# A layer of Fourier attention and a quantized feed-forward: another order of the opening, and one constant made on the chip

## The reference

```python
x = x + attn(layernorm(x), W_q, W_kv, W_o)        # x: 4 x 512 rows of 512
x = x + ffn(layernorm(x), gate_w, up_w, down_w, gate_scale, up_scale, down_scale)

def attn(x, W_q, W_kv, W_o):                      # 16 heads of 32
    qf  = l2_normalize(fft((x @ W_q.T).reshape(B, S, 16, 32)))
    kvf = l2_normalize(fft((x @ W_kv.T).reshape(B, S, 16, 32)))
    kvf = cumsum(kvf, axis=1)                     # over the rows
    return ifft(qf * kvf).real.reshape(B, S, 512) @ W_o.T

def ffn(x, ...):                                  # 512 -> 1536 -> 512, weights cast to fp8
    fuse = silu(x @ q(gate_w) * gate_scale) * (x @ q(up_w) * up_scale)
    return fuse @ q(down_w) * down_scale
```

## Time and profile before

| | us |
|---|---|
| median of 3 runs | 419.12 |
| lowest and highest | 418.77, 419.37 |
| the profiled execution | 419.79 |
| its span in the trace | 418.0 |

### The profile page before, as it was taken

How to read it: one execution, slowest core, us unless ns; L and a number is a source line. 1 busy time by engine, 2 the same in 40 slices (tenths; PEclk the granted TensorE clock), 3 DMA queues, 4 the chain that set the end, 5 groups by cost and what they waited for, 6 DMA issues and landing times.

```text
span 418.0 us, 5504 instructions
## 1 busy us (share of the span) xinstructions
PE 408.8 (98%) x1897; PEld 202.8 (49%) x1897; DVE 297.4 (71%) x514; ACT 193.2 (46%) x323; POOL 108.2 (26%) x114
## 2 busy tenths in 40 slices
PE   7999999999999999999999999999999999999994
PEld 3744454445555554454555555454444444444442
DVE  4998998999999699997984972167865854422234
ACT  3687756587736245445242563255442441131220
POOL 0133551015154137043541012032461001300003
PEclk9999999999999999999999999999999999999998
DMA  8986546600181143232112014411112051200002
GB/s 249 264 267 239 163 117 162 149 17 2 38 256 36 26 77 71 57 127 74 28 26 50 2 29 101 72 50 53 26 26 52 0 77 25 100 2 0 2 0 101
DMA packets 57547, 33.55 MB, mean 80 GB/s; under 512 B 49456, under 2 KB 49840, under 8 KB 57392
## 3 DMA queue, kind: packets, MB, share of 16 engines
q1 hardware_dynamic: 57088, 32.93, 30.3%
q10 hardware_dynamic: 432, 0.28, 0.2%
HBM read 17.44 MB, written 4.19 MB: 52 GB/s over the span
## 4 chain that ended last, share of the span: by engine, by line
PE 89%; DMA 3%; DVE 3%; ACT 2%; POOL 1%; SPq 1%; issue 1%; POOLq 0%; DVEq 0%
PE bd L488 20%; PE bu L470 19%; PE bg L470 19%; PE ba L370 14%; PE ba L415 8%; PE bd L370 3%; DMA h<-x_dram 1%; PE ba L388 1%; PE bd L415 1%; DMA hT<-w_q_dram 1%; PE bd L388 1%; PE bd L356 1%; PE bu L415 1%; POOL xs L1603 1%; PE bg L447 0%
## 5 line engine op out<-in xcount | busy, mean ns | idle before, releaser
L470 PE MATMUL bu<-hT,gu 128*128 128x512 f16 x384 | 90.7, 379 | 0.0
L470 PE MATMUL bg<-hT,gu 128*128 128x512 f16 x376 | 89.0, 379 | 0.0
L1234 DVE SCALAR_TENSOR_TENSOR ff<-bu,us,sl 128x512 f32<-128x512 f32 x48 | 35.9, 748 | 56.0 <-PE bu L470 52.8
L741 ACT ACTIVATE sl<-bg,gs 128x512 f32<-128x512 f32 x48 | 32.9, 686 | 78.0 <-PE bg L470 77.0
L370 PE MATMUL ba<-wf,xT 128*128 128x512 f16 x288 | 63.2, 379 | 0.0
L470 PEld LDWEIGHTS bu<-hT,gu 128*128 128x128 f16 x384 | 37.5, 98 | 45.5 <-DVE ff L1234 0.6
L470 PEld LDWEIGHTS bg<-hT,gu 128*128 128x128 f16 x376 | 35.6, 98 | 44.9 <-issue 4.1
L488 PE MATMUL bd<-dw,fu 128*128 128x512 f32 x192 | 51.1, 411 | 0.0
L1634 POOL TENSOR_TENSOR h<-ff,h 128x512 f32<-128x512 f32 x14 | 17.5, 1272 | 122.2 <-DVE ff L1265 122.2
L370 PEld LDWEIGHTS ba<-wf,xT 128*128 128x128 f16 x288 | 27.9, 98 | 34.1 <-issue 1.1
L488 PE MATMUL bd<-own,half 128*128 128x512 f16 x184 | 43.0, 379 | 0.0
(11 more groups left out here) (201 smaller groups left out, 524.3 us busy)
## 6 DMA issues: line engine op xcount, KB each, us to landing
h<-x_dram SPq DMA_DIRECT2D x16, 256.0 KB, 4.2
out_dram<-h SPq DMA_DIRECT2D x15, 256.0 KB, 2.0
hT<-w_q_dram SPq DMA_DIRECT2D x4, 256.0 KB, 5.0
gu<-w_kv_dram SPq DMA_DIRECT2D x4, 256.0 KB, 4.4
hT<-gate_w_dram SPq DMA_DIRECT2D x2, 512.0 KB, 3.5
hT<-up_w_dram SPq DMA_DIRECT2D x2, 512.0 KB, 5.6
gu<-woT_dram SPq DMA_DIRECT2D x1, 1024.0 KB, 5.1
hT<-down_w_dram SPq DMA_DIRECT2D x2, 512.0 KB, 4.9
```

Of the source, the lines that this page charges most:

```text
L470: m = e.matmul(bk[:, :], gu[:, c, 4 * w + k, col:col + P], hT[:, b % 2, part, k, :], start=k == 0 and part == 0, stop=k == KT - 1 and part ...
L741: e.activation(sl[:, n % 2, :], bg[:, :], ACT.Silu, scale=gs[:, i:i + 1]).then_inc(a_silu, 1)
L1234: e.scalar_tensor_tensor(out=ff[:, n % 2, :], in0=bu[:, :], scalar=(us if b < HALF else us2)[:, i:i + 1], in1=sl[:, n % 2, :], op0=ALU.mul ...
```

## The change

- **TensorE** folds the second query block ahead of `heads(0, 1)`; the last two query blocks are folded together, bank by bank (`pe_fold_last`), so that banks become complete one after the other. Two key blocks are folded ahead of `heads(1, 1)`. The warm-ups become 14, 3, 3, 3 and 3 instead of 14, 3 and 4.
- **VectorE** takes the second pair's scaling ahead of tile 1's statistics, and the sums and scalings of the key weights, with the low parts of the query weights, ahead of `xn(0, 1)` and of tile 2's statistics. It writes the constant `heads` with five memsets (`dve_heads`); `fwd` alone is read from memory.
- **ScalarE** sums block 5 and copies the first folded bank ahead of tile 1's root; `act_xh(0, 1)` goes behind the sum of block 7. A wait is added for a buffer of `act_sum_w`.
- **SyncE** issues x's tile 2 behind all blocks of the key weights, whose last two change places; the constant's transfer is 64 KB instead of 128 KB.

```diff
-            return 7 * w + KT + k
+            return 10 + k if w else 3 + k

             if j == 0:
-                e.wait_ge(d_cst, 16)
+                e.wait_ge(v_heads, 5)

+        def pe_fold_last(e):
+            for f in (2, 3):
+                e.wait_ge(v_head, 3 + f)
+            for k in range(KT):
+                for f in (2, 3):
+                    m = e.matmul(ba[AT["fold", 0, k]][:, P * f:P * f + P], raw[0][:, f, P * k:P * k + P], fs[:, f, :],
+                                 start=True, stop=True)
+                m.then_inc(s_fold, 1)

@@ tensor_program
             pe_heads(e, 0, 0)
             pe_warm(e, 3)
             pe_fold(e, 0, 0)
+            pe_fold(e, 0, 1)
             pe_heads(e, 0, 1)
-            pe_warm(e, 4)
-            pe_fold(e, 0, 1)
-            pe_fold(e, 0, 2)
-            pe_fold(e, 0, 3)
+            pe_warm(e, 3)
+            pe_fold_last(e)
             pe_heads(e, 1, 0)
             pe_qk(e, 0, 0, 0)
-            pe_heads(e, 1, 1)
+            pe_warm(e, 3)
             pe_fold(e, 1, 0)
             pe_fold(e, 1, 1)
+            pe_heads(e, 1, 1)
+            pe_warm(e, 3)
             pe_fold(e, 1, 2)
             pe_fold(e, 1, 3)
             pe_qk(e, 0, 1, 0)

@@ act_sum_w
+            if j > KT:
+                e.wait_ge(*summed(j - KT))

@@ scalar_program
             act_sum_w(e, 3)
+            act_sum_w(e, 5)
+            act_wf(e, 0, 0)
             act_root0(e, 0, [1])
-            act_sum_w(e, 5)
-            act_xh(e, 0, 1)
-            act_wf(e, 0, 0)
             act_wf(e, 0, 1)
             act_wf(e, 0, 2)
             act_wf(e, 0, 3)
             act_sum_w(e, 7)
+            act_xh(e, 0, 1)
             act_root0(e, 0, [2])

@@ dve_head
+            if j == 0:
+                e.wait_ge(d_cst, 16)

+        def dve_heads(e):
+            e.memset(heads, 0.0).then_inc(v_heads, 1)
+            e.wait_ge(v_heads, 1)
+            for q in range(4):
+                r = slice(HD * q, HD * q + HD)
+                e.memset(cst[r, 128 + HD * q:128 + HD * q + HD], 1.0 / UNIT).then_inc(v_heads, 1)

@@ vector_program
             dve_zero(e)
+            dve_heads(e)
...
             dve_sum_w(e, 2)
+            dve_head(e, 0, 1)
             dve_stats1(e, 0, 1)
             dve_root0_head(e, 0, [1])
-            dve_head(e, 0, 1)
+            dve_wf(e, 0, 0)
+            dve_wf(e, 0, 1)
+            dve_sum_w(e, 4)
+            dve_wf(e, 0, 2)
+            dve_wf(e, 0, 3)
+            dve_head(e, 1, 0)
             dve_root0_tail(e, 0, [1])
             dve_xn(e, 0, 1)
+            dve_sum_w(e, 6)
+            dve_head(e, 1, 1)
             dve_stats1(e, 0, 2)
-            dve_sum_w(e, 4)
-            dve_wf(e, 0, 0)
-            dve_wf(e, 0, 1)
-            dve_wf(e, 0, 2)
-            dve_wf(e, 0, 3)
-            dve_sum_w(e, 6)
-            dve_head(e, 1, 0)
+            dve_root0_head(e, 0, [2])
             dve_stats1(e, 0, 3)
-            dve_root0_head(e, 0, [2])
-            dve_head(e, 1, 1)
             dve_root0_tail(e, 0, [2])

@@ sp_cst
-            e.dma_start(cst[:, 0:256], cst_d).then_inc(d_cst, 16)
+            e.dma_start(fwd, cst_d).then_inc(d_cst, 16)

@@ sync_program
             sp_raw(e, 1, 1)
-            sp_x(e, 0, 2)
             sp_raw(e, 1, 0)
             sp_xT(e, 0, 0)
+            sp_raw(e, 1, 3)
             sp_raw(e, 1, 2)
-            sp_raw(e, 1, 3)
+            sp_x(e, 0, 2)
             sp_ident(e)
```

More of the change, by code:

```diff
@@ L40, in constants @@
         inv[r, r] = np.concatenate([ire, iim], 1)
-    heads = np.kron(np.eye(4), np.ones((HD, HD))) / 2.0 ** 14
     ident = np.eye(P)
@@ L44, in constants @@
     ones = np.ones((P, P))
-    return (np.concatenate([fwd, heads, ident], 1).astype(np.float32),
+    return (np.concatenate([fwd, ident], 1).astype(np.float32),
             np.concatenate([inv, tri, ones], 1).astype(np.float32))
+UNIT = 2.0 ** 14
 NPR = 18
@@ L197, in build @@
         a_zh, v_zl = sem("act_zh"), sem("dve_zl")
+        v_heads = sem("dve_heads")
         v_most, s_bound, a_bound, v_unit2, v_gus, p_dw = (
@@ L1929 @@
         "ds": np.ascontiguousarray(L0_ffn_down_scale),
-        "cst": np.ascontiguousarray(cst[:, 0:2 * P]),
+        "cst": np.ascontiguousarray(cst[:, 0:P]),
         "cst2": cst2,
-        "ident": np.ascontiguousarray(cst[:, 2 * P:]),
+        "ident": np.ascontiguousarray(cst[:, P:]),
     }
```

## The result

| | before | after |
|---|---|---|
| median of 4 runs, us | 418.94 | 423.82 |
| lowest and highest | 418.40, 419.37 | 423.46, 424.41 |
| the profiled execution | 419.79 | 424.41 |
| its span | 418.0 | 422.6 |

The kernel is slower by a ratio of 1.0104 (95% interval 1.0083 to 1.0125), some 4.4 us; the forecast was 422.4 in a range of 420.3 to 424.6. The two medians in the table lie 4.9 us apart: the ratios given here with an interval are estimated from the single executions and are not quotients of two medians. A second set, six executions of the kernel after beside 23 of the kernel before, gave 423.16 against 419.31, ratio 1.0098 (1.0076 to 1.0120).

What follows compares the result with a forecast made beforehand. TensorE, busy 98% of the span, was taken to bound the kernel. Terms 0.1 + 1.3 + 0.15 + 1.2 + 0.7 = 3.45, taken as 3.3, turned the 419.12 median into 422.4 us, range 420.3 to 424.6.

Steps and rivals of the forecast that it cites:

- Step 1: Opening transfers and constants: extra memsets and the halved constant transfer change nothing, 0 us (bounds 0 and -2.2).
- Step 2: Up to the first product: earlier banks, but `heads(1,0)` waits for a key-weight sum; `qk(0,0,0)` at 14.68, +0.1 us.
- Step 3: Six warm-up matmuls behind `qk(0,0,0)`, where TensorE had no gap, cost 6 x 0.216 = +1.30 us.
- Step 4: Second pair's scale: VectorE waits for TensorE's late `heads(1,1)`; `qk(0,1,0)` at 22.41 instead of 20.95, +1.46 so far.
- Step 5: VectorE's late low parts of w_kv make TensorE stand 0.73 and 0.45 us before `qk(0,2,0)`: +1.2 us.
- Step 6: Later: x tile 3's transpose and the scaled output weight pass VectorE's and ScalarE's lag to TensorE, +0.7 us.
- (a): Rival: only the warm-up matmuls cost, VectorE catches up, later waits vanish; 420.5 us, chance 0.13.
- (b): Rival: TensorE's clock falls in the gap from 13.1 to 14.5, slowing `qk(0,0,0)` by 2.5 us; 424.9, chance 0.06.
- (c): Rival: smaller constant lets w_q's second block land earlier, opening up to 1.75 us sooner; 418.3 at best, chance 0.03.
- (d): Rival: nothing measurable moves, since w_kv block 0's sum comes earlier and `qk(0,0,0)` starts at 13.4; 419.2, chance 0.04.

Runs made afterwards that it cites:

- const_alone: Kernel before with the constant `heads` written by VectorE and its transfer 64 KB, nothing else: 420.05 against 419.31 us, ratio 1.0008.
- no_warm: Kernel after without the six warm-up matmuls behind `qk(0,0,0)`: 423.19 against 420.05 us for before, ratio 1.0077.
- reordered: Kernel after without the six later warm-ups, several VectorE and ScalarE calls put back, `heads(1,1)` between first two key folds: 419.58 against 419.31 us for before, ratio 1.0013.
- heads_early_no_warm: Kernel after with `heads(1,1)` right behind `qk(0,0,0)` and without the six warm-ups there: 422.80 against 420.05 us for before, ratio 1.0064.
- heads_early: Kernel after with `heads(1,1)` moved up right behind `qk(0,0,0)`, all warm-ups kept: 422.56 against 420.05 us for before, ratio 1.0059.
- before_warm6: Kernel before with six warm-up matmuls added, three behind `heads(1,1)` and three behind `fold(1,1)`: 421.73 against 420.05 us, ratio 1.0036.
- before_again: Kernel before, unchanged, run once more for a second trace: 418.25 us in one execution, 23 others between 418.20 and 421.07.
- after_again: Kernel after, unchanged, run once more: 423.16 against 419.31 us for before, ratio 1.0098.

## Why the prediction was right, step by step

**What bounds the kernel.** Held: where the time went could be read from TensorE's starts at the same products, in every kernel here.

**Step 1, transfers and constants, 0.** Held, by const_alone. The trace has no wait for w_kv's blocks nor for x tile 2 on the path.

**Step 2, +0.1.** Right mechanism, mis-sized: `g1` is 7.61 in both traces of after, against 7.11 and 7.04, so +0.5, just outside the bounds of -0.4 to +0.4. The sum of block 4 at 13.55 and `heads(1,0)` directly behind it stand where they were placed. The 0.4 us are small pieces of one chain: counted from `heads(0,0)`, `fold_last` starts 4.06 us on instead of 3.84, the first low part 5.41 instead of 5.15, the sum ends at 7.29 instead of 7.02, and the product follows 0.32 after that instead of 0.20. So the four links of this chain took 0.22, 0.04, 0.01 and 0.12 us more than the lengths and starts of the trace before gave. In the absolute times this was hidden, since `heads(0,0)` came 0.52 earlier by chance: 14.55 against the 14.68 worked out. That the first product came out so near was luck. The fold bank by bank, alone, wins 0.5. With the sum of block 4 and several other calls put back `g1` falls by 1.3 (7.53 in no_warm against 6.22 in reordered); the two together give +0.8 where +0.5 was measured. What the place of the sum costs by itself no run shows.

**Step 3, +1.30.** Held as a term: 1.5 us alone. But "nothing there is idle" holds only for the kernel before: in the kernel after 0.65 of it is on the path, and the second three stand where TensorE would have waited for `fs` all the same, as no_warm shows. The total of steps 3 and 4 was right, its division between warm-ups and waits only in part.

**Step 4, `qk(0,1,0)` at 22.41.** Held: 22.32, and from `qk(0,0,0)` 7.77 us instead of the 7.73 worked out. (Its +1.46 is 0.06 above steps 2 and 3, where the sum at the end has 0.15; the difference is small.) VectorE's reciprocal is at 19.88 (20.1), `heads(1,1)` at 19.56 (19.70). The transpose was in time, but only just (issued at 18.6, landed 3.6 us later, 22.2): where the product could start earlier (heads_early_no_warm, reordered) it stands 0.52 and 0.55.

**Step 5, +1.2.** Held: from `qk(0,1,0)` to `qk(0,2,0)` it is 8.93 us against 7.77, +1.16, and `qk(0,2,0)` is at 31.25 (31.4). The two waits stand where they were placed, and both vanish in heads_early, whose VectorE is 1.7 us earlier at that point.

**Step 6, +0.7.** Held, with a spread: `g3` grew by 1.09 in the first pair of traces and by 0.59 in the second, and by 0.84 between the means. Both chains that the step names can be seen. Tile 3's first product starts 5.32 us after `qk(0,2,0)` in both traces of before, and 5.70 and 5.82 us after it in the two of after. Timelines of TensorE, before and after:

```profile
34.04 2.75 PE L370 MATMUL bg<-wf,xT 128*128 128x512 f16 x12
```

```profile
36.95 2.75 PE L383 MATMUL bg<-wf,xT 128*128 128x512 f16 x12
```

In the first trace of after the second transpose of tile 3 is issued at 34.4 and lands 2.4 us later, 36.8, just ahead of that product: +0.38, as the step has it. In the second TensorE first stands 0.26 us for the size of the output weights, which landed 5.9 us after their issue: +0.50 in all. The rest is mostly the output weight's wait, 0.99 in the first trace and 0.20 in the second, against 0.41 and none before, and it is not the chain of step 6 alone: in the first trace VectorE stood 1.05 us at 43.71 for a tile of x, in the second it did not.

**What lies behind 48.78.** I had it unchanged. `rest` grew by 0.98 in the profiled pair, but by 0.07 in the second, and over the kernels here it lies between 372.8 and 374.9 with no order in it: the trace of before is the lowest. One source is visible, a wait of TensorE near 100 us that is absent in some traces and 1.00 us in others (timeline of TensorE, before_warm6 and after):

```profile
101.89 1.89 PE L470 MATMUL bg<-hT,gu 128*128 128x512 f16 x8 [1.00 <-ACT sl L743]
```

```profile
103.81 1.89 PE L483 MATMUL bg<-hT,gu 128*128 128x512 f16 x8 [0.18 <-ACT sl L757]
```

In the trace of before it is absent, so it accounts for 0.18 of the 0.98 us. Where the others lie stays open.

**The rivals.** (a) would have had `g2` grow by 1.3 alone; it grew by 2.55. (b): the gap was there, 1.31 us, and the clock did not fall. (c): the block of w_q landed 0.5 us earlier, by chance. (d): the sum of block 4 ended at 14.23, behind two low parts, as its place in the order says.

**The total.** The result lies 1.4 us above the forecast of 422.4, within the range. The forecast was +3.3, from a sum of 3.45 that was lowered for idle time which no row shows. The spans grew by 4.6 us in both pairs of traces, in different ways: `g1` +0.50, `g2` +2.55, `g3` +1.09, `rest` +0.98 and `heads(0,0)` 0.52 earlier in the first; +0.57, +2.55, +0.59, +0.07 and 0.82 later in the second. What the prediction worked out is `g2`, +2.65 by its sum, with 0.1 ahead of it and 0.7 behind. That part repeats and was right; the start of `heads(0,0)` and `rest` were left at nothing and differ from one execution to the next, and that both totals come to 4.6 is chance. Between the sets the difference of the medians was 4.9 us and 3.9 us, so about 1 us of the miss can't be told from that spread.

## What to carry to other kernels

An operation that another engine's whole queue waits for must be issued first, not where its own engine has room: here a 0.3 us pair of matmuls behind two folds held VectorE for 2.6 us, and the loss came out at three later places. Before a wait is taken away, list what is late next with its slack: the gains of about 1 us in reordered and heads_early went, wholly or in large part, to a transpose and to a transfer whose slack was smaller than that. And a warm-up belongs only in a gap: behind a full queue it costs its own length.

## What the runs showed of the hardware

- The same 256 KB transfer, at the same place in the queue, took 3.1 to 4.9 us from issue to landing in different executions; the start of the first dependent matmul moved between 5.94 and 7.46 us with it and with the warm-ups.
- The 14 warm-ups that open the kernel take between 4.65 us (after) and 6.07 us (no_warm), depending on when their spacing falls from 0.43 to 0.22 us. The granted clock reads 1.00 all the while, so at the start of the span that row does not show why the spacing is twice what it is later; the time of the block follows the spacing.
- TensorE standing 1.82 us was followed by a stretch at the lower clock, to 11 us, in one trace; 1.66 and 1.31 us were not, in others. These traces don't say what decides.
- The 1 MB transfer of the output weights took longer where the transfers ahead of it were issued closer to it. From the issue of `down_w` to its own it was 8.0 us in before and before_again, and it landed after 5.1 and 5.3 us; 6.8 in after and after_again, 5.3 and 5.9; 5.2 and 5.4 in heads_early and heads_early_no_warm, 7.2 and 7.5. The traces show the two together; no run shows that one causes the other.
